# Block ends without GpSimd's drain, attention denominators inverted in node rows, and ends of layers reordered by unit

## What is computed

```python
x = _layernorm(x + _L0_gnn_ref(x, ...))   # relational convolution, 2 passes over the edges
x = _layernorm(x + _L1_gnn_ref(x, ...))   # graph convolution, 1 pass
x = _layernorm(x + _L2_gnn_ref(x, ...))   # graph attention, 2 passes, 8 heads of 16 numbers
x = _layernorm(x + _L3_gnn_ref(x, ...))   # tensor-product convolution, 1 pass
# _layernorm: (x - mean) / sqrt(var + 1e-5) over the 128 numbers of a row
# attention: ex = exp(e - max over the edges of a node)
#            out = segment_sum(ex / segment_sum(ex)[dst] * h[src]) + bias
```

## Time and profile before

| | us |
|---|---|
| median of 3 runs (9771.4 to 9777.08) | 9772.5 |
| the profiled execution | 9753.1 |
| its span, first to last instruction | 9751.4 |
| POOL busy | 6753.4 (69%) |
| PE busy | 7087.4 (73%) |
| DVE busy | 5963.3 (61%) |
| ACT busy | 3173.0 (33%) |

### The profile page before, as it was taken

The page is one execution under the profiler, slowest core; times in us unless marked ns, Lnnn a source line. Parts: engine busy times, 40 slices in busy tenths (PEclk is TensorE's granted clock), DMA queues, the critical chain, the costliest instruction groups (busy, mean ns, idle before and its releaser), DMA issues. The chain is left out here.

```text
span 9751.4 us, 159349 instructions
## 1 busy us (share of the span) xinstructions
PE 7087.4 (73%) x35262; PEld 5033.3 (52%) x35262; DVE 5963.3 (61%) x20485; ACT 3173.0 (33%) x10688; POOL 6753.4 (69%) x7058
## 2 busy tenths in 40 slices
PE   3555554666677666669999957777477777699999
PEld 2222223433343344334444456566466666599999
DVE  8455553444434444446665557777677777699887
ACT  1222220000011000000000045555455555599998
POOL 0777777777734777767777667777477777377775
PEclk9999997555577555555555567777777777799999
DMA  3222223111134111111111122222222222211112
GB/s 86 85 81 85 81 84 97 53 53 53 53 148 166 53 53 53 53 52 53 53 53 53 47 60 60 60 60 60 45 60 60 60 60 59 72 53 53 53 52 49
DMA packets 293240, 638.44 MB, mean 65 GB/s; under 512 B 125198, under 2 KB 161169, under 8 KB 280353
## 3 DMA queue, kind: packets, MB, share of 16 engines
q0 software_dynamic: 224928, 422.56, 16.8%
q1 hardware_dynamic: 67744, 210.12, 6.3%
HBM read 481.33 MB, written 150.87 MB: 65 GB/s over the span
## 5 line engine op out<-in xcount | busy, mean ns | idle before, releaser
L1054 POOL DMA_INDIRECT relsum_rows<-relation_table,tab_idx x1994 | 1889.4, 948 | 849.3 <-issue 489.4
L1097 PE MATMUL relsum_sums<-relsum_hot,relsum_rows 128*128 128x128 f32 x3988 | 1557.5, 499 | 928.7 <-DMA relsum_rows<-relation_table,tab_idx 681.6
L1097 PEld LDWEIGHTS relsum_sums<-relsum_hot,relsum_rows 128*128 128x128 f32 x3988 | 995.7, 312 | 1487.7 <-DMA relsum_rows<-relation_table,tab_idx 1475.2
L997 POOL DMA_INDIRECT conv_rows<-tensor_table,src_idx x1008 | 954.1, 946 | 457.5 <-issue 217.6
L664 POOL DMA_INDIRECT records<-sort_recs,place_rows x968 | 987.2, 1020 | 295.1 <-issue 295.1
L1054 POOL DMA_INDIRECT gcnsum_rows<-x_table,src_idx x997 | 953.5, 956 | 341.8 <-PE gcnsum_sums L1097 157.3
L997 POOL DMA_INDIRECT gat1sum_rows<-gat_table,src_idx x1008 | 954.3, 947 | 307.2 <-issue 228.3
L997 POOL DMA_INDIRECT gat2sum_rows<-gat_table,src_idx x1008 | 953.3, 946 | 307.2 <-issue 224.0
L1064 DVE TENSOR_SCALAR relsum_hot<-iota_row,dst_rel,w 128x128 f32<-128x128 f32 x1994 | 707.8, 356 | 427.6 <-issue 419.4
L1097 PE MATMUL gcnsum_sums<-gcnsum_hot,gcnsum_rows 128*128 128x128 f32 x1994 | 783.0, 496 | 0.0
L1755 PE MATMUL gat1sum_sums<-gat1sum_hot,gat1sum_scaled 128*128 128x128 f32 x2016 | 587.9, 383 | 265.5 <-DVE gat1sum_scaled L1686 257.9
(11 more groups left out here) (378 smaller groups left out, 15134.5 us busy)
## 6 DMA issues: line engine op xcount, KB each, us to landing
relation_table<-table_row SPq DMA_DIRECT2D x30, 2048.0 KB, 6.3
relation_table<-sort_space SPq DMA_DIRECT2D x40, 1024.0 KB
relsum_rows<-relation_table,tab_idx POOLq DMA_INDIRECT x1994, 2.5
place_lo_wide<-lo_rows SPq DMA_DIRECT2D x121, 256.0 KB, 3.4
relation_table<-place_extra SPq DMA_DIRECT2D x20, 1024.0 KB
gat1sum_rows<-gat_table,src_idx POOLq DMA_INDIRECT x1008, 2.5
gat2sum_rows<-gat_table,src_idx POOLq DMA_INDIRECT x1008, 2.5
conv_rows<-tensor_table,src_idx POOLq DMA_INDIRECT x1008
```

What stands on the lines that cost most here:

```text
L997: pool.indirect_dma_start(bufs[:, t % depth, :], None, table, bass.IndirectOffsetOnAxis(ap=idx[:, t:t + 1], axis=0)).then_inc(landed[t % l ...
L1054: pool.indirect_dma_start(rows[:, t % depth, :], None, table, bass.IndirectOffsetOnAxis(ap=idx[:, t:t + 1], axis=0)).then_inc(landed[t % d ...
L1097: pe.matmul(bank[:, 0:P], rows[:, t % depth, :], hot[:, t % HOTS, :], start=True, stop=True).then_inc(s["multiplied"], 1)
```

## The change

Every block is opened with `nc.Block(no_gpsimd_drain=True)`. The rest of the diff, cut to what acts:

```diff
-def finish_layer(env, tag, how, table=None, weights=None, width=None, scale=None, store_x=None):
+def finish_layer(env, tag, how, table, weights=None, width=None, scale=None):
...
+        taken_by_dve = [u for u in range(UNITS) if u >= UNITS - 2 or (scale is not None and u % 2)]
...
             for u in range(UNITS):
+                if u + 4 < UNITS:
+                    make(u + 4)
                 if weights is not None:
                     turn_x(u)
-                if u + 4 < UNITS:
-                    make(u + 4)
-                if weights is not None and u:
-                    apply(u - 1)
+                    if u:
+                        apply(u - 1)
...
# VectorE
+            if how.updates:
+                update(0)
+                update(1)
             for g in range(PAIRS):
+                measure(2 * g)
+                measure(2 * g + 1)
+                if how.updates and g + 1 < PAIRS:
+                    update(2 * g + 2)
                 dve.drain()
                 find_spread(dve, env, pair_blocks(g)).then_inc(s["measured"], 1)
-                if g:
-                    dve.wait_ge(s["rooted"], g)
-                    find_shift(dve, env, pair_blocks(g - 1)).then_inc(s["shifted"], 1)
+                if how.updates and g + 1 < PAIRS:
+                    update(2 * g + 3)
+                dve.wait_ge(s["rooted"], g + 1)
+                find_shift(dve, env, pair_blocks(g)).then_inc(s["shifted"], 1)
+                if weights is not None and 2 * g - 3 in taken_by_dve:
+                    take(2 * g - 3)
+            # then VectorE normalises the last unit itself, and takes the units left to it
...
# ScalarE
+            root(0)
+            for u in range(UNITS + 1):
+                if u % 2 and u // 2 + 1 < PAIRS:
+                    root(u // 2 + 1)
+                if u < UNITS - 1:
+                    norm(u)
+                if weights is not None:
+                    if u:
+                        keep(u - 1)
+                    if u >= 2 and u - 2 not in taken_by_dve:
+                        take(u - 2)
...
# SyncE stores the last pair as two units

# attend: only in the first attention pass, after VectorE's memset of acc
+            if added_to_x is not None:
+                x = env.x[:, 0:BLKS, :]
+                dve.tensor_tensor(x, x, over_rows(added_to_x, BLKS), ALU.add)
...
-def divide_sums(dve, acc, pair): ...
-def floor_sums(dve, acc): ...
+def pick_denominators(pe, env, acc, to):
+    for b in range(BLKS):
+        mm = pe.matmul(to[:, b * HEADS:(b + 1) * HEADS], acc[:, 1, b * P:(b + 1) * P], env.ident[:, 0:P:CH], start=True, stop=True)
+    return mm
+def invert_denominators(dve, frm, to):
+    dve.tensor_scalar(to, frm, 1e-30, None, ALU.max)
+    dve.drain()
+    return dve.reciprocal(to, to)
...
# between_attentions, per unit u of 384 columns:
+                # ScalarE widen:  act.copy(wide[:, u % 3, :, :], over_columns(own, CH))
+                # TensorE spread: pe.transpose(spread_ps[u % 3][...], pe_in, env.ident[:, :])  x3
+                # VectorE:        mean = acc[:, 0, ...] * spread_ps[u % 3]
+                # ScalarE:        hidden = Relu(mean + gat_bias1)
+                # TensorE apply:  3 matmuls with gat_w[1]; VectorE take: copy of 432 columns
-            pool.tensor_tensor(x, x, over_rows(env.gat_bias2[:, :], BLKS), ALU.add)
...
# AttentionEnd.update (gatout), per unit:
+        dve.tensor_tensor(self.mean[:, u % 2, :, :], made[:, 0:UNIT * P].rearrange("p (g c) -> p g c", c=CH),
+                          over_columns(inverse, CH), ALU.mult)
+        dve.drain()
+        return dve.tensor_tensor(x, x, self.mean[:, u % 2, :, :], ALU.add)
```

More of the change, by code:

```diff
@@ L1172, in finish_layer, with before_norm, out_rows, wait_taken @@
         s = {n: env.sig(f"{tag}_{n}").sem for n in (
[L1173 to L1176, removed]
+            "made", "freed", "measured", "rooted", "shifted", "normed", "normed_last", "turned", "kept", "applied", "taken", "taken_dve", "stored")}
+        block = ctx.enter_context(nc.Block(no_gpsimd_drain=True))
         freed = s["freed" if how.updates else "normed"]
+        taken_by_dve = [u for u in range(UNITS) if u >= UNITS - 2 or (scale is not None and u % 2)]
+        taken_by_act = [u for u in range(UNITS) if u not in taken_by_dve]
         def pair_blocks(g):
             return slice(2 * g * UNIT, 2 * (g + 1) * UNIT)
[L1182 to L1194, removed]
+        def before_norm(u, k, b):
+            return env.x[:, b, :] if how.updates else made[u % 4][:, k * P:(k + 1) * P]
+        def out_rows(u):
+            return rows[:, u * UNIT:(u + 1) * UNIT, :], out[u % 2][:, 0:UNIT * width].rearrange("p (b f) -> p b f", b=UNIT)
+        def wait_taken(eng, u):
+            if u in taken_by_dve:
+                eng.wait_ge(s["taken_dve"], taken_by_dve.index(u) + 1)
+            else:
+                eng.wait_ge(s["taken"], taken_by_act.index(u) + 1)
         @block.tensor
@@ L1261, in _, with norm @@
+            last.then_inc(s["normed_last"], 1)
+            if weights is not None:
+                for u in taken_by_dve:
+                    if u > UNITS - 4:
+                        take(u)
         @block.scalar
         def _(act):
[L1263 to L1270, removed]
+            def norm(u):
+                act.wait_ge(s["shifted"], u // 2 + 1)
+                for k, b in enumerate(unit_blocks(u)):
+                    last = act.activation(env.x[:, b, :], before_norm(u, k, b), ACT.Identity, bias=env.shift[:, b:b + 1],
+                                          scale=env.rstd[:, b:b + 1])
+                last.then_inc(s["normed"], 1)
@@ L1276, in keep, with root, take @@
                 act.copy(x_t[:, u % 2, :], turn[u % 2][:, 0:UNIT * P]).then_inc(s["kept"], 1)
-            how.act_first(act)
[L1279 to L1291, removed]
+            def root(g):
+                act.wait_ge(s["measured"], g + 1)
+                own = pair_blocks(g)
+                act.activation(env.rstd[:, own], env.rstd[:, own], ACT.Sqrt, bias=env.eps[:, 0:1]).then_inc(s["rooted"], 1)
+            def take(u):
+                act.wait_ge(s["applied"], u + 1)
+                to, frm = out_rows(u)
+                if scale is None:
+                    act.copy(to, frm).then_inc(s["taken"], 1)
+                    return
+                for k, b in enumerate(unit_blocks(u)):
+                    last = act.activation(to[:, k, :], frm[:, k, :], ACT.Identity, scale=scale[:, b:b + 1])
+                last.then_inc(s["taken"], 1)
+            how.act_first(act)
+            root(0)
[4 more added lines that the diff above has]
+                    norm(u)
+                if weights is not None:
+                    if u:
+                        keep(u - 1)
+                    if u >= 2 and u - 2 not in taken_by_dve:
+                        take(u - 2)
         @block.sync
@@ L1833, in _, with out_rows, spread, apply @@
+        block = ctx.enter_context(nc.Block(no_gpsimd_drain=True))
+        def out_rows(u):
+            return rows[:, u * UNIT:(u + 1) * UNIT, :].rearrange("p b f -> p (b f)"), out[u % 4][:, 0:UNIT * width]
         @block.tensor
         def _(pe):
[L1835 to L1836 removed]
+            def spread(u):
+                pe.wait_ge(s["widened"], u + 1)
+                if u >= 3:
+                    pe.wait_ge(s["divided"], u - 2)
+                for k in range(UNIT):
+                    pe_in = wide[:, u % 3, k * HEADS:(k + 1) * HEADS, :].rearrange("p h c -> p (h c)")
+                    mm = pe.transpose(spread_ps[u % 3][:, k * P:(k + 1) * P], pe_in, env.ident[:, :])
+                mm.then_inc(s["spread"], 1)
+            def apply(u):
+                pe.wait_ge(s["hidden"], u + 1)
```

269 lines of the change are left out of this document (147 added, 122 removed).

## The result

The changed kernel takes 9689.2 us (median of 4 runs, 9685.6 to 9690.2) against 9774.1 us before (4 runs, 9771.4 to 9777.1): ratio 0.991, interval 0.9895 to 0.993. The first rival, "the drains don't come back", named 9698.

The account below looks back on a forecast made before the run. GpSimd's gathers were taken to pace the long passes, untouched by the change. Node stages -57.2, drains +22.5 and gat1sum +2.9 gave -31.8 us, from 9772.5 to 9741 us; range 9692 to 9762.

Parts of the forecast that it names:

- The first rival: own_signals: line 97's drain stays at 0.03 to 0.2 us, so 20 us are saved; 9698 us, chance 0.2.
- Where the drains come back: own_signals, line 97: the first drain after gathers takes 8.5 us in five places, 42.5 us lost.
- The other drains: Block ends: GpSimd drains left out save 11.5 us after both relsums and gcnsum, and 8.5 after place_edges.
- relout: Node stage relout: cycles of 4.0 us from root to root instead of 5.14; gain 4.2 us (3.5 to 5).
- gcnout: Node stage gcnout: 47.2 us become 37.1, with three cycles averaging 6.0; gain 10 us (7 to 13.4).
- between_attentions: Stage between_attentions: 44.1 us to the last copy become 28, within 25 to 43; gain 16 us (1 to 20).
- gatout: Node stage gatout: 75.1 us become 50.1, with picking 10 and inverse 2.2; gain 25 us (19 to 32).
- tpout: End of node stage tpout: 4.72 us of norm on ScalarE become 2.4; gain 2 us (1.5 to 2.5).
- near 1.0 was the sign: between_attentions: TensorE's clock grant, PEclk, was to show near 1.0 if the forecast held.
- The lower-clock rival: Node stages: TensorE stays at its lower clock, they gain only 32 us; 9766 us, no measurable change, chance 0.1.
- gat1sum's 2.9 us: gat1sum: the bias add moved there holds up one gather and costs 2.9 us (0 to 4.2).
- The sign for being wrong by slower passes: Second relsum or gat2sum growing by more than 5 us would show the forecast wrong.

Follow-up runs that it names:

- experiment 6: The kernel before with only GpSimd's drains left out at all block ends, on the third set's chip: 9741.3 against 9761.4 us, ratio 0.998.
- experiment 5: The changed kernel rerun without and with GpSimd's block-end drains put back: 11344.9 and 11351.1 us in the second set, 9674.7 and 9697.1 in the third set.
- third set: Four follow-up kernels on a chip of its own with even gathers: kernel before 9761.4 us, changed kernel 9674.7 (0.9911).
- second set: Four follow-up kernels on another chip, with over a hundred gathers of each pass late: kernel before 11432 us, changed kernel 11344.9 (0.9925).

## Why the prediction was wrong

**The failed step is "Where the drains come back".** It charged 5 x 8.5 = 42.5 us to line 97; their median of 0.12 makes 0.6 us for all five. The evidence of the earlier trace rows was set aside because none of its six drains came first behind gathers, and place_edges' drain (line 484) was taken as the nearest case. It was nearest in place and not in kind: line 97's is the one that goes with the clearing of semaphores, line 484's a plain one. The bounds of the step, 0.03 to 8.6, did hold the truth, but the range of the whole was cut near the first rival's number: 9692 is 6 us below 9698. With the node stages at the dear end of their own bounds (72.9 us) that rival reaches 9682.5, and the measured 9689 lies inside.

**The other drains were right.** 11.5 + 8.5 = 20.0 us forecast, 20.1 (experiment 6) and 22.4 (experiment 5) measured on even gathers.

**The terms of the node stages**, forecast and measured from window to window: relout 4.2 and 4.5, gcnout 10 and 14.7, between_attentions 16 and 15.4, gatout 25 and 26.6, tpout 2 and 1.0; in sum 57.2 and 62.2.

gcnout is the term that was mis-sized most. Its rows after the change:
```profile
5576.22 0.87 DVE L1502 SCALAR_TENSOR_TENSOR x<-gcnout_made,gcnout_dinv,x 128x128 f32<-128x128 f32 x3 [0.76 <-PE gcnout_made L1497]
...
5585.22 0.30 ACT L1299 ACTIVATE rstd<-rstd,eps 128x6 f32<-128x6 f32 x1 [1.59 <-DVE rstd L1120]
...
5592.20 0.30 ACT L1299 ACTIVATE rstd<-rstd,eps 128x6 f32<-128x6 f32 x1 [2.58 <-DVE rstd L1120]
...
5597.59 0.30 ACT L1299 ACTIVATE rstd<-rstd,eps 128x6 f32<-128x6 f32 x1 [1.22 <-DVE rstd L1120]
...
5601.66 0.30 ACT L1299 ACTIVATE rstd<-rstd,eps 128x6 f32<-128x6 f32 x1
...
5608.51 0.61 DVE L1248 COPY gcnout_rows<-gcnout_out 128x432 f32<-128x432 f32 x1 [0.32 <-PE gcnout_out L1213]
```
To the second root 9.0 us (forecast 10.1), then cycles of 7.0, 5.4 and 4.1, in sum 16.4 (18.0), then 7.5 to the end of the last take (9.0). Each part is shorter by 1 to 1.6 us. In the first cycle TensorE's granted clock was 0.59, near its lower level (0.50 is 1.2 GHz), in the other two 1.00 and 0.94, the upper. gatout shows it too: the same three cycles took 16.7 us, the end 6.8 for 9.3. What ate some of that is its picking of denominators:
```profile
8297.93 12.94 PE L1810 MATMUL gatout_out<-ident,acc 128*128 128x8 f32 x60 [2.88 <-PEq L98]
...
8323.21 0.30 ACT L1299 ACTIVATE rstd<-rstd,eps 128x6 f32<-128x6 f32 x1 [1.89 <-DVE rstd L1120]
...
8339.93 0.30 ACT L1299 ACTIVATE rstd<-rstd,eps 128x6 f32<-128x6 f32 x1
...
8345.43 1.25 DVE L1250 TENSOR_TENSOR gatout_rows<-gatout_out,attr 128x384 f32<-128x384 f32 x2 [0.58 <-PE gatout_out L1213]
```
12.9 us where 10 were taken, near the dear bound of 13.1, at a granted clock of 0.50.

**between_attentions came out right in part by luck.** The prediction wanted TensorE at its upper level throughout, for which its own terms give 6.5 + 2.2 + 3 + 12.5 = 24.2 us; it took 28 and did not say what the rest was for. TensorE does not stay there: PEclk is 0.73 for the stage, where near 1.0 was the sign, and 0.58 for the sixty denominators, which take 11.4 us and not 6.5. Most of the units behind them run near the upper level (0.93 from 6958.0 to 6969.5), one every 1.07 us where 1.25 were taken:
```profile
6940.96 11.42 PE L1810 MATMUL between_den<-ident,acc 128*128 128x8 f32 x60 [2.42 <-PEq L1521]
...
6962.31 0.54 DVE L1883 TENSOR_TENSOR between_mean<-acc,between_spread 128x384 f32<-128x384 f32 x1
...
6963.38 0.54 DVE L1883 TENSOR_TENSOR between_mean<-acc,between_spread 128x384 f32<-128x384 f32 x1
...
6968.85 0.61 DVE L1875 COPY between_rows<-between_out 128x432 f32<-128x432 f32 x1 [0.43 <-PE between_out L1859]
```
To the end of the last copy it is 28.8 us from the window's start, forecast 28.

**relout was right as worked out**, cycle for cycle. Three of the roots:
```profile
4290.27 0.30 ACT L1299 ACTIVATE rstd<-rstd,eps 128x6 f32<-128x6 f32 x1 [0.91 <-DVE rstd L1120]
...
4294.22 0.30 ACT L1299 ACTIVATE rstd<-rstd,eps 128x6 f32<-128x6 f32 x1 [1.55 <-DVE rstd L1120]
...
4298.16 0.30 ACT L1299 ACTIVATE rstd<-rstd,eps 128x6 f32<-128x6 f32 x1 [1.55 <-DVE rstd L1120]
```
3.95 us from root to root, forecast 4.0.

**tpout** gained 1 us less than forecast: its end did shrink, but the same 270 matmuls were busy for 32.0 us where they had been for 30.5, at a grant of 0.89 for 0.90. On the third set it gained 2.7 us (43.7 to 41.0, with matmuls busy for 32.2 us in both), so the forecast of 2 lies between the two.

**The lower-clock rival** is out: the grant rose in four of the five stages. **gat1sum's 2.9 us** were right. The sign for being wrong by slower passes did not show: from barrier to barrier the second relsum took 1257.0 us before, with its drain's 4.2, and 1257.1 after, gat2sum 1322.3 and 1324.1.

**The sum.** With the terms as measured: 62.2 + 20.0 - 2.9 = 79.3 us of gain. Less the 15.7 us of the longer passes that makes 63.6, for the 64.7 between the first two traces. The timed gain was 85 in the first comparison and 86.7 in the third set, with an interval of some 16 us to either side. Most of the 6 to 7 us between lie in the node stages. In the third set the kernel of experiment 6 and the changed kernel, both without drains, differ by the rest of the change alone. Their spans are 66.2 us apart, their medians 66.6, and their windows 28.5, 56.1, 48.3, 79.1, 43.7 against 23.9, 40.7, 31.9, 51.1, 41.0: 67.1 us less, where the first two traces have 62.2. So one stage's window, with the same code, differs by up to 1.7 us between two executions (tpout of the kernel before: 42.0 and 43.7). With 67.1 the sum is 84.3 of the 86.7; the last 2.4 are not explained.

## What to carry to other kernels

Two instructions of one name can differ in cost (0.17 and 8.6 us here): before a deferred wait is charged somewhere, look for what else the instruction there does, and when a row of that very place contradicts the reasoning, let the range reach the row's end in full. A drain that is last in its block costs only what it is later than the next slowest engine; whether it is last depends on how evenly the gathers' rows arrive. And taking work off an engine that shares something with the critical one (GpSimd's add beside VectorE's floor) can bring as much as a better algorithm.

## What was not expected of the hardware

- GpSimd's plain drain behind indirect DMAs costs up to 8.6 us, and still 8.0 us 65 us after the last of them; the one that goes with the clearing of a range of semaphores costs 0.07 to 0.17 us, straight behind them, and a plain one after that 0.04. What makes the plain one 2.3 us in two places and 7 to 8.6 in three was not found.
- The median duration of a gather is 944 or 947 ns. The changed kernel has 947 in two traces and 944 in the third, and one chip shows both, so neither the kernel nor the chip decides it. Over the six thousand gathers that moves the whole by about 16 us, as much as a small change. One profiled execution against another must be read with this in mind.
- On two of the three sets' chips over a hundred gathers of each pass of a thousand came late, and the kernel took 17 % longer, at the same two median durations. The page of the changed kernel in the second set shows it as idle time, 1193.8 us before relsum's gathers:
```profile
L1054 POOL DMA_INDIRECT relsum_rows<-relation_table,tab_idx x1994 | 1889.5, 948 | 1193.8 <-issue 496.3
```
  By the same group in the first profile of after it was 838.1.
